# Five tables for the last two attention layers of a graph network kernel: the order of four engines and the dealing of PSUM slots written anew

## The reference, cut to what matters

```python
for l in range(2):
    q = (x @ Wq[l] + bq[l]).reshape(N, 8, 64)     # k and v alike
    a = (q[dst] * k[src]).sum(-1) * scale         # per edge
    e = jnp.exp(a - amax[dst])
    alpha = e / (denom[dst] + 1e-16)
    agg = segment_sum(alpha[:, :, None] * v[src], dst).reshape(N, 512)
    x = agg + (x @ Ws[l] + bs[l]) + enc
# then: layer norm, relu(x @ W1 + b1) @ W2 + b2 + x, layer norm, + enc
```

## Time and profile before

| what | value |
|---|---|
| median of 3 runs | 1119.63 us (1119.62 to 1119.72) |
| profiled execution: first to last instruction | 1117.2 us |
| PE matmul / weight load busy | 95% / 88% of the span |
| DVE / POOL / ACT busy | 69% / 60% / 52% |
| first attention layer of the last block | from 784.20 us |
| second attention layer | from 919.67 us |
| last scaling of the first / second layer ends | 901.20 / 1036.51 us |

### The profile page before, as it was taken

How to read it: one execution, slowest core, us unless ns; L and a number is a source line. 1 busy time by engine, 2 the same in 40 slices (tenths; PEclk the granted TensorE clock), 3 DMA queues, 4 the chain that set the end, 5 groups by cost and what they waited for, 6 DMA issues and landing times.

```text
span 1117.2 us, 20722 instructions
## 1 busy us (share of the span) xinstructions
PE 1066.1 (95%) x6808; PEld 987.7 (88%) x6808; DVE 773.4 (69%) x1535; ACT 577.6 (52%) x1032; POOL 673.3 (60%) x923
## 2 busy tenths in 40 slices
PE   7999999899999999999999999999999999999797
PEld 7899897699888999889998899987999879998795
DVE  7899867756658566575665756666778867777634
ACT  7999675455321553315543145433667637676340
POOL 3232447754577545875558755499656866478671
PEclk9999999999999999999999999999999999999899
DMA  5200011412021120211201212122201201021101
GB/s 129 31 1 1 7 38 58 149 58 86 1 86 49 58 86 1 78 56 59 86 1 55 78 48 77 69 83 75 66 1 43 71 4 45 1 76 39 38 1 46
DMA packets 40963, 56.92 MB, mean 51 GB/s; under 512 B 14312, under 2 KB 14812, under 8 KB 40735
## 3 DMA queue, kind: packets, MB, share of 16 engines
q1 hardware_dynamic: 40600, 55.37, 15.7%
q10 hardware_dynamic: 260, 0.21, 0.1%
HBM read 51.44 MB, written 4.12 MB: 50 GB/s over the span
## 4 chain that ended last, share of the span: by engine, by line
PE 79%; DVE 6%; POOL 5%; ACT 4%; issue 3%; DMA 2%; DVEq 0%; POOLq 0%; SPq 0%; PEldq 0%; ACTq 0%
PE ps L340 42%; PE ps L1768 8%; PE ps L362 8%; PE ps L786 5%; PE ps L2101 3%; PE ps L2028 3%; PE ps L2402 3%; POOL w_lo L380 2%; ACT away L737 1%; PE ps L2065 1%; PE ps L1259 1%; PE ps L1246 1%; PE ps L1742 1%; DMA w_raw<-L_gnn_wk 1%; PE ps L1220 1%
## 5 line engine op out<-in xcount | busy, mean ns | idle before, releaser
L380 POOL TENSOR_TENSOR w_lo<-w_raw,w_hi 128x512 fp32r<-128x512 f32 x152 | 204.8, 1348 | 12.7
L340 PE MATMUL ps<-yt_hi,w_hi 128*128 128x314 f32 (+2 forms) x640 | 201.8, 315 | 2.8 <-DVE yt_lo L2236 1.6
L340 PE MATMUL ps<-yt_hi,w_lo 128*128 128x314 f32 (+2 forms) x640 | 197.6, 309 | 0.0
L340 PE MATMUL ps<-yt_lo,w_hi 128*128 128x314 f32 (+2 forms) x640 | 197.3, 308 | 0.0
L459 POOL TENSOR_SCALAR prob<-prob,rinv 125x628 f32<-125x628 f32 x160 | 126.4, 792 | 105.2 <-DVE rinv L444 86.9
L403 ACT ACTIVATE pt_hi<-ps 125x625 fp32r<-125x625 f32 x160 | 109.2, 694 | 102.9 <-PE ps L362 101.7
L377 POOL TENSOR_SCALAR w_hi<-w_raw 128x512 fp32r<-128x512 f32 x152 | 97.7, 643 | 95.3 <-DMA w_raw<-L_gnn_wo 28.8
L340 PEld LDWEIGHTS ps<-yt_hi,w_hi 128*128 128x128 f32 x640 | 121.8, 190 | 5.9 <-issue 4.4
L340 PEld LDWEIGHTS ps<-yt_hi,w_lo 128*128 128x128 f32 x640 | 121.7, 190 | 0.0
L340 PEld LDWEIGHTS ps<-yt_lo,w_hi 128*128 128x128 f32 x640 | 121.5, 190 | 0.1
L786 PE MATMUL ps<-oh_s,oh_d 125*125 125x314 bf16 x800 | 111.4, 301 | 10.1 <-DVE oh_s L639 6.8
(11 more groups left out here) (325 smaller groups left out, 2787.2 us busy)
## 6 DMA issues: line engine op xcount, KB each, us to landing
w_raw<-L_gnn_m_w SPq DMA_DIRECT2D x8, 1024.0 KB, 5.4
w_raw<-L_gnn_W SPq DMA_DIRECT2D x6, 1024.0 KB, 5.4
w_raw<-L_gnn_wv SPq DMA_DIRECT2D x4, 1024.0 KB, 6.1
w_raw<-L_gnn_wq SPq DMA_DIRECT2D x4, 1024.0 KB, 5.4
...
```

Source lines behind the costliest of these rows:

```text
L340: ins = pe.matmul(out_ap, lhs(i, kk), rhs(j, kk), start=kk == 0 and n == 0, stop=kk == count - 1 and n == 2)
L380: pool.tensor_tensor(w[slot][1][:, kk, 0:cols], w_raw[slot][:, kk, 0:cols], w[slot][0][:, kk, 0:cols].bitcast(FP32), ALU.subtract).then_in ...
```

## The change

The tables `LAYER_PE`, `LAYER_DVE`, `LAYER_ACT` and `LAYER_POOL` hold the same names in another order, and `LAYER_PE` has 121 `-` where it had 18, so that the four PSUM slots are dealt otherwise. No operation is added or taken away, and no code changes. Both layers use the same tables. All lines below the first table stand two lines further down in the changed kernel (L379 for L377). The diff, cut:

```diff
 LAYER_PE = """
-q0.0 q0.1 k0.0 k0.1 q1.0 s0_0 s0_1 q1.1 s0_2 - s0_3 t0_0 k1.0 s0_4 t0_1 s1_0 - k1.1 s1_1 t0_2 s1_2 - w0.0 w0.1
+- - q0.0 q0.1 k0.0 k0.1 q1.0 q1.1 s0_0 - s0_1 - - s0_2 - - k1.0 - s0_3 k1.1 - - s0_4 - t0_0 - - w0.0 - - t0_2 -
...
 LAYER_POOL = """
-spw0 spw1 scale:s0_0 scale:s0_1 spw2 scale:s0_2 spw3 scale:s0_3 scale:s0_4 scale:s1_0 scale:s1_1 scale:s1_2
+spw0 spw1 spw2 spw3 scale:s0_0 scale:s0_1 scale:s0_2 scale:s0_3 scale:s0_4 scale:s1_0 scale:s1_1 scale:s1_2
...
-scale:s3_3 scale:s3_4 scale:s4_0 scale:s4_1 scale:s4_2 scale:s4_3 scale:s4_4 spq0 spq1 scale:s5_0 scale:s5_1
-scale:s5_2 scale:s5_3 spk0 spk1 scale:s5_4 scale:s6_0 spv0 spv1 scale:s6_1 scale:s6_2 scale:s6_3 scale:s6_4
-scale:s7_0 scale:s7_1 scale:s7_2 scale:s7_3 scale:s7_4 spv2 spv3 spq2 spq3 spk2 spk3
+scale:s3_3 scale:s3_4 scale:s4_0 scale:s4_1 scale:s4_2 spq0 spq1 scale:s4_3 scale:s4_4 scale:s5_0 scale:s5_1
+scale:s5_2 scale:s5_3 spv0 spv1 scale:s5_4 scale:s6_0 spv2 scale:s6_1 scale:s6_2 scale:s6_3 scale:s6_4
+scale:s7_0 scale:s7_1 scale:s7_2 scale:s7_3 scale:s7_4 spv3 spk0 spk1 spk2 spq2 spq3 spk3
```

More of the change, by code:

```diff
@@ L179 @@
-s7_0 pv5.1 t6_1 t6_2 s7_1 t6_3 s7_2 t6_4 s7_3 s7_4 pv6.0 t7_0 t7_1 pv6.1 t7_2 - t7_3 t7_4 pv7.0 pv7.1 v0.0
-v3.0 v0.1 v1.0 v1.1 v2.0 v2.1 v4.0 v3.1 v4.1
+- - q0.0 q0.1 k0.0 k0.1 q1.0 q1.1 s0_0 - s0_1 - - s0_2 - - k1.0 - s0_3 k1.1 - - s0_4 - t0_0 - - w0.0 - - t0_2 -
+- t0_1 - - s1_0 w0.1 - s1_1 - - t0_3 - - s1_2 - - t0_4 - - s1_3 - pv0.0 - s1_4 - - t1_0 pv0.1 - t1_1 - - s2_0 -
+- q2.0 - - t1_2 - t1_3 s2_1 q2.1 s2_2 - - t1_4 - - pv1.0 - s2_3 - - k2.0 pv1.1 - t2_0 - - t2_1 k2.1 - s2_4 - -
+t2_2 - - s3_0 - w1.0 w1.1 - - s3_1 - t2_3 s3_2 - t2_4 - - s3_3 - - pv2.0 t3_0 - s3_4 - - t3_1 pv2.1 - - s4_0 -
@@ L181 @@
+s4_1 - - q3.0 - - t3_2 - t3_3 q3.1 s4_2 - - t3_4 - s4_3 - - pv3.0 pv3.1 - - t4_1 - w2.0 - - t4_0 - s4_4 w2.1
+s5_0 - - w3.0 t4_2 s5_1 s5_2 w3.1 - - t4_3 t4_4 - s5_3 - - k3.0 - s5_4 k3.1 - - pv4.0 - t5_0 - - s6_0 pv4.1 -
+t5_1 - s6_1 t5_2 - s6_2 t5_3 - t5_4 - - pv5.0 - s6_3 - - s6_4 - t6_0 - - s7_0 pv5.1 - - t6_1 s7_1 t6_2 s7_2 -
+t6_3 - - s7_3 - t6_4 s7_4 - pv6.0 - - t7_0 pv6.1 - t7_1 t7_2 t7_3 t7_4 pv7.0 v0.0 pv7.1 v3.0 v1.0 v0.1 v2.0 v1.1
+v2.1 v3.1 v4.0 v4.1
 """.split()
 LAYER_DVE = """
-lo:q0e lo:q0o lo:k0e sc:s0_0 lo:k0o sc:s0_1 sc:s0_2 sc:s0_3 lo:q1e lo:q1o lo:t0_0 sc:s0_4 lo:t0_1 sc:s1_0
@@ L184 @@
[L184 to L188, removed]
@@ L189 @@
-lo:t5_2 lo:t5_3 sc:s6_2 sc:s6_3 lo:t5_4 sc:s6_4 sc:s7_0 lo:t6_0 acp:5 lo:t6_2 lo:t6_1 sc:s7_1 lo:t6_3 sc:s7_2
-sc:s7_3 lo:t6_4 sc:s7_4 xl:1 lo:t7_0 acp:6 lo:t7_1 lo:t7_2 lo:t7_3 lo:t7_4 xl:2 acp:7 xl:3 vb:v0 vb:v1 vl:v0
-vb:v2 vl:v1 vb:v3 vl:v2 vl:v3 vb:v4 vl:v4
+lo:q0e lo:k0e lo:k0o lo:q0o sc:s0_0 sc:s0_1 lo:q1e sc:s0_2 lo:q1o sc:s0_3 sc:s0_4 lo:k1e lo:k1o lo:t0_0 lo:t0_2
+lo:t0_1 sc:s1_0 acw:0 sc:s1_1 sc:s1_2 sc:s1_3 lo:t0_3 lo:t0_4 sc:s1_4 lo:t1_0 acp:0 sc:s2_0 lo:t1_1 lo:t1_2
+sc:s2_1 lo:t1_3 sc:s2_2 lo:t1_4 lo:q2e lo:q2o sc:s2_3 acp:1 lo:t2_0 lo:t2_1 sc:s2_4 lo:k2e lo:t2_2 lo:k2o
@@ new lines @@
+sc:s3_0 acw:1 sc:s3_1 sc:s3_2 sc:s3_3 lo:t2_3 lo:t2_4 lo:t3_0 sc:s3_4 lo:t3_1 sc:s4_0 sc:s4_1 acp:2 lo:t3_3
+lo:t3_2 sc:s4_2 lo:t3_4 lo:q3e sc:s4_3 acp:3 lo:q3o lo:t4_1 sc:s4_4 sc:s5_0 lo:t4_0 acw:2 sc:s5_1 sc:s5_2
+lo:t4_2 acw:3 lo:t4_3 sc:s5_3 lo:t4_4 sc:s5_4 lo:k3e lo:k3o sc:s6_0 lo:t5_0 acp:4 sc:s6_1 lo:t5_1 lo:t5_2
+sc:s6_2 lo:t5_4 lo:t5_3 sc:s6_3 sc:s6_4 sc:s7_0 lo:t6_0 acp:5 sc:s7_1 lo:t6_1 lo:t6_2 sc:s7_2 lo:t6_3 sc:s7_3
+lo:t6_4 sc:s7_4 xl:0 lo:t7_0 acp:6 lo:t7_1 lo:t7_2 xl:1 xl:2 lo:t7_3 lo:t7_4 acp:7 xl:3 vb:v0 vl:v0 vb:v1 vb:v2
@@ L192 @@
+vl:v1 vb:v3 vl:v2 vb:v4 vl:v3 vl:v4
 """.split()
 LAYER_ACT = """
[L194 to L202, removed]
+hi:q0e hi:q0o du:q0e hi:k0e hi:k0o hi:q1e hi:q1o exp:s0_0 du:q0o exp:s0_1 du:q1o exp:s0_2 hi:k1e hi:k1o hi:t0_0
+exp:s0_3 hi:t0_2 hi:t0_1 exp:s0_4 du:q1e exp:s1_0 hi:t0_3 hi:t0_4 exp:s1_1 exp:s1_2 exp:s1_3 hi:t1_0 hi:t1_1
@@ new lines @@
+exp:s1_4 hi:t1_2 exp:s2_0 hi:t1_3 exp:s2_1 hi:q2o hi:t1_4 du:q2o hi:q2e exp:s2_2 exp:s2_3 hi:t2_0 hi:t2_1 hi:k2e
+hi:t2_2 hi:k2o exp:s2_4 du:q2e exp:s3_0 hi:t2_3 exp:s3_1 hi:t2_4 exp:s3_2 exp:s3_3 hi:t3_0 hi:t3_1 exp:s3_4
+exp:s4_0 exp:s4_1 hi:t3_2 hi:t3_3 hi:q3e hi:t3_4 exp:s4_2 hi:q3o hi:t4_1 exp:s4_3 du:q3e du:q3o hi:t4_0 exp:s4_4
+hi:t4_2 exp:s5_0 exp:s5_1 exp:s5_2 hi:t4_3 hi:t4_4 exp:s5_3 exp:s5_4 hi:k3e hi:k3o hi:t5_0 xh:0 exp:s6_0 xh:1
+hi:t5_1 hi:t5_2 exp:s6_1 hi:t5_4 hi:t5_3 exp:s6_2 exp:s6_3 hi:t6_0 exp:s6_4 hi:t6_1 exp:s7_0 hi:t6_2 exp:s7_1
@@ L203 @@
+hi:t6_3 hi:t6_4 exp:s7_2 exp:s7_3 hi:t7_0 xh:2 exp:s7_4 hi:t7_1 hi:t7_2 hi:t7_3 hi:t7_4 xh:3 vh:v0 vh:v1 vh:v2
+vh:v3 vh:v4
 """.split()
 LAYER_POOL = """
-spw0 spw1 scale:s0_0 scale:s0_1 spw2 scale:s0_2 spw3 scale:s0_3 scale:s0_4 scale:s1_0 scale:s1_1 scale:s1_2
+spw0 spw1 spw2 spw3 scale:s0_0 scale:s0_1 scale:s0_2 scale:s0_3 scale:s0_4 scale:s1_0 scale:s1_1 scale:s1_2
 scale:s1_3 scale:s1_4 scale:s2_0 scale:s2_1 scale:s2_2 scale:s2_3 scale:s2_4 scale:s3_0 scale:s3_1 scale:s3_2
-scale:s3_3 scale:s3_4 scale:s4_0 scale:s4_1 scale:s4_2 scale:s4_3 scale:s4_4 spq0 spq1 scale:s5_0 scale:s5_1
```

## The result

| | before | after |
|---|---|---|
| median, us | 1119.69 (5 executions, 1119.62 to 1122.95) | 1131.89 (5 executions, 1130.23 to 1133.12) |
| span of the profiled execution, us | 1117.2 | 1128.4 (of the run of 1130.23) |

The ratio after / before is 1.0103, with a 95% interval of 1.0092 to 1.0114: 12.2 us slower. Predicted were 1129.1 us, slower, with 1122.5 to 1135 as the range.

A forecast was written before the change was run, and what follows sets the result against it. PE paces each layer until projections run out behind w3, then POOL's list. Late Wv costs 8.4 and 8.7 us, less 3.5 and 3.6 ahead of pv4.0 and 0.5 at the first layer's end: +9.5, giving 1129.1 us, range 1122.5 to 1135.

The forecast's parts named there:

- The late load: SP's queue: Wv is issued only behind k3 and Wk, lands 8.2 us later, so spv0 begins at T + 9.1.
- T: Mark in each layer: the start of pv4.0, forecast about 85.3 us into each layer.
- Behind it: POOL after the wait for Wv: last scaling at T + 36.5, costing 8.4 and 8.7 us; PE stands 8.5 us.
- Ahead of T: PE before pv4.0: idle time of 4.3 and 4.4 us falls to 0.8, gaining 3.5 and 3.6 us.
- The Ws and Wq pieces: POOL's pieces moved ahead of the first scaling and of s4_3: PE's work or later slack hides them, cost nothing.
- the last layer's extra piece: POOL, end of the last layer: one piece more is left, k pieces ready some 4 us later, cost nothing.
- The layer's end: First layer, behind the last scaling: v0.0 waits for one piece, not two, gaining 0.5 us.
- The sum: First layer +4.4, second +5.1, together +9.5 on the span 1117.2: 1126.7; median 2.4 above, 1129.1 us.
- A: Rival, SP's waits: their order does not matter, last scaling 8.9 us sooner in each layer, 1111.3 us; chance 0.07.
- B: Rival, behind the stall: PE at its lower clock bounds, not POOL; 2 us per layer, 1133 us; chance 0.10.
- C: Rival, loads of Wk and Wv: the two overlap fully, 1123.5 us; chance 0.07.

The follow-up runs named there:

- e1: The changed kernel with SP's wait for w3 and load of Wv (last layer: W2) ahead of those for k3 and Wk: 1116.38 us, ratio 0.9967.
- e4: The kernel before, with SP's wait ahead of the load of Wv (last layer: W2) put on pv4 instead of w3: 1130.21 us, ratio 1.0076.
- e7: The kernel before, with POOL's pieces spk0 and spk1 moved from behind the scaling of s5_3 to behind the last scaling: 1119.95 us, ratio 1.0.
- e3: The changed kernel with 48 extra matmuls in each layer where PE stands idle ahead of t5_4: 1131.82 us, ratio 1.0099.
- e5: The kernel of e1 with DVE's subtractions xl:0, xl:1 and xl:2 moved behind lo:t7_4: 1119.6 us, ratio 1.0.
- e6: The kernel of e1 with POOL's piece spv2 moved from behind the scaling of s6_0 to behind the last scaling: 1116.22 us, ratio 0.9965.

## Why the prediction was right, and where its sizes were off

**The late load.** Right in mechanism and size. Wk and Wv went out 0.43 us apart (forecast 0.45), Wv landed after 8.2 (8.2), and spv0 began at T + 9.02 (9.1), in the second layer at T + 8.68. e1 takes the wait away and with it 15.3 of 15.5 us. The estimate from the Trainium skill's "DMA: Bandwidth & Descriptors" put both matrices 6.8 us behind the first issue; measured are 8.65 (871.30 + 8.22 less 870.87). The page's fixed time is fitted to DMAs that GpSimd issues, and these are issued by SP; and its section Bandwidth says that between HBM and SBUF about 358 GB/s binds, by which the same sum would be 7.9 us, an estimate, still 0.8 short.

**Behind it.** The scaling of s5_4 ends at 884.71 + 0.79, T + 14.8 (forecast 15.4), the last at T + 36.56 and T + 35.47 (forecast 36.5 for both). In the first layer a scaling took 1.34 instead of 0.79, POOL waited 0.28 once more, and spv0 began 0.34 later behind T than in the second layer: together 1.2, for the 1.1 between them. e4 shows a loss of the same kind, 4.1 and 3.9 us, without the new tables. PE stood for 6.93 us, not 8.5: there is about 1 us more of PE work between T and t5_4 than the sum of the durations, and s5_4 was 0.6 us sooner.

**Ahead of T.** This term was mis-sized. Forecast was T at +85.3, a gain of 3.5 and 3.6 us; measured +86.46 in both layers, 2.4 and 2.4. The step that was wrong is "PE idles 4.3 and 4.4 us ahead of T": 84.5 us was a sum of durations of whole pieces, and PE needs more. The stretches over this part, of before and then of after, show it:

```profile
784.20:873.00 88.80, 86.56 (x614) 84.73 (x613) 67.12 (x114) 59.17 (x107) 56.96 (x103) 1.00 0.14 45
```
```profile
784.20:870.60 86.40, 86.19 (x614) 84.67 (x613) 66.72 (x115) 59.31 (x107) 55.06 (x100) 1.00 0.10 34
```

The same 614 records are 86.2 to 86.6 us of PE, not 84.5. Idle were 2.2 us before, and 0.2 are after; the other 0.4 of the gain is in the records themselves, since one outlasts the start of the next and so covers a short wait. Where the 1.7 us between the sum and the records lie is not shown. The 2.2 us of before were nearly all in four waits, by the waits of PE in 784.2 to 873 us (total, times, longest):

```profile
PE ps L362 <- DVE acc L1973: 0.8, 1, 0.8
PE ps L362 <- POOL prob L459: 0.5, 1, 0.5
PE ps L2101 <- DVE low L429: 0.5, 1, 0.5
PE ps L2101 <- DVE q_o_low L1950: 0.3, 1, 0.3
```

After, no such wait is left, and T is 86.4 to 86.5 us behind the second layer's start in every kernel with the new tables, 88.8 to 88.9 in e4 and e7, which have the old order of PE. That the new tables would take nearly all was right; how much there was, one more row of the kernel before would have told. How much of it the order won and how much the dealing of slots, no run separates.

**The Ws and Wq pieces, and the last layer's extra piece.** They were costed at nothing, and it was so: PE has no wait left ahead of T, and the end behind the last scaling is 80.76 against 80.70.

**The layer's end.** Forecast 0.5 us gained, measured none (18.47 both). The one piece that v0.0 waits for took 1.17 + 1.71 us instead of 0.62 + 1.29, which is 1.0 longer, beside two of DVE's subtractions, and v0.0 followed at 910.27, 0.1 us after its end. Before, such a stretch stood there too, but smaller: the second of the two pieces took 0.62 + 1.72. That this is what used up the forecast 0.5 is worked out from these times and not tested.

**The sum.** On the span, forecast 1126.7, measured 1128.4. The 1.7 are 1.1 + 1.1 ahead of T and 0.5 at the layer's end, less 1.0 for the second layer's last scaling; that the errors partly cancel is luck. The other 1.1 of the 2.8 between 1129.1 and 1131.89 is the distance from span to median, 3.5 us where I carried over 2.4. In each run that lists both, the time is about 1.8 us above the span; the rest depends on which execution was traced, and after's was the fastest of its five.

**The rivals.** A falls: the order of SP's waits mattered. Its kernel is e1, which came to 1116.3 and not to 1111.3, since there were 2.4 us per layer to be had ahead of T and not 3.5, the first layer's last scaling came at T + 29.12 and not + 27.6, and its end took 19.05 us and not 18.0. B falls by e3 for the stretch up to the last scaling; its low clock is real and costs where PE paces (e5). C falls by the second landing of 8.2 us. The reason given for A's 8.9 us per layer, that POOL gets through its list by T + 27.6, held in the second layer and missed the first by two stretched operations, which are gone in e5.

**Still open.** With the load in time, POOL and the chain over DVE and ACT bound the last scaling within 1.2 us of each other (e6 took 1.9 us from POOL and won 0.7 in the second layer), and in the first layer v0.0 and the clock behind it come on top (e5, e6); no run separates them further.
